# Expert stage of a decoder kernel: the transpose of a block's token rows placed directly ahead of the matmuls that read it

## The reference

```
choices = top 2 of 8 of (normed x) @ router_logits        # per token
gate_out = x_of_expert @ gating_einsum[e]                 # 512 -> 2 x 512
activation = gelu(gate_out[:, 0]) * gate_out[:, 1]
expert_outputs = activation @ linear[e] * per_expert_scale[e]
out = sum over the 2 chosen experts of weight * expert_outputs
```

## Time and profile before

| | us |
|---|---|
| median of 3 runs (2063.98 to 2066.97) | 2065.59 |
| the profiled execution's own time | 2066.97 |
| its span, first to last instruction | 2065.2 |
| TensorE busy | 1872.6 (91%) |
| VectorE busy | 1022.1 (49%) |
| ScalarE busy | 593.3 (29%) |
| expert blocks, from the first transposes to the last `dn` matmul | 1101.84 to about 1337.9 |

### The profile page before, as it was taken

How to read it: one execution, slowest core, us unless ns; L and a number is a source line. 1 busy time by engine, 2 the same in 40 slices (tenths; PEclk the granted TensorE clock), 3 DMA queues, 4 the chain that set the end, 5 groups by cost and what they waited for, 6 DMA issues and landing times.

```text
span 2065.2 us, 29153 instructions
## 1 busy us (share of the span) xinstructions
PE 1872.6 (91%) x11802; PEld 1218.9 (59%) x11802; DVE 1022.1 (49%) x1888; ACT 593.3 (29%) x1899; POOL 391.7 (19%) x456
## 2 busy tenths in 40 slices
PE   6799999999999999999866999958999999989898
PEld 5575656645666665665655888745766744434344
DVE  3555655426556655666730011046444543534599
ACT  0313222405455454555510111102122121212411
POOL 3332322320010110110011000052211200000488
PEclk9899999999999999999767999978999999999999
DMA  9000002000000000001045888740000205432010
GB/s 374 11 1 1 1 1 97 1 23 16 1 16 16 2 16 16 1 16 62 1 159 196 342 331 329 265 144 1 1 1 1 107 36 227 176 133 112 0 37 36
DMA packets 30821, 170.70 MB, mean 83 GB/s; under 512 B 3832, under 2 KB 3832, under 8 KB 17024
## 3 DMA queue, kind: packets, MB, share of 16 engines
q1 hardware_dynamic: 28128, 161.50, 20.7%
q0 software_dynamic: 2560, 7.34, 1.2%
HBM read 155.98 MB, written 16.52 MB: 84 GB/s over the span
## 4 chain that ended last, share of the span: by engine, by line
PE 74%; DVE 12%; issue 4%; DMA 4%; ACT 3%; POOL 3%; SPq 0%; POOLq 0%; DVEq 0%
PE PS L1109 7%; PE PS L897 6%; PE PS L946 5%; PE PS L1189 5%; PE PS L1149 5%; PE PS L986 4%; PE PS L977 4%; PE PS L1219 4%; PE PS L1118 3%; PE PS L954 2%; DMA R<-in_ctx 2%; PE PS L1009 2%; PE PS L1025 2%; PE PS L1045 2%; PE PS L1250 2%
## 5 line engine op out<-in xcount | busy, mean ns | idle before, releaser
L1987 POOL TENSOR_TENSOR rstd<-veps,mhalf 112x1 f32<-112x1 f32 (+1 forms) x76 | 57.6, 759 | 697.7 <-DVE veps L1279 683.4
L1109 PEld LDWEIGHTS PS<-R,W 128*128 128x128 f32 x1344 | 154.9, 194 | 11.6 <-issue 11.6
L1405 DVE TENSOR_REDUCE nmx<-PS 112x2 f32<-112x750 f32 x128 | 114.1, 933 | 91.6 <-PE PS L1009 91.6
L1109 PE MATMUL PS<-R,W 128*128 128x128 f32 x1344 | 155.2, 277 | 1.9 <-issue 1.9
L1808 ACT ACTIVATE R<-PS,small 112x112 f32<-112x112 f32 x256 | 87.0, 378 | 230.7 <-DVE small L1318 230.7
L1856 ACT ACTIVATE R<-PS,nmx 112x375 f32<-112x375 f32 x256 | 143.0, 575 | 1.3 <-DVE nmx L1405 1.3
L897 PE MATMUL PS<-xT,W 128*128 128x224 f32 x640 | 126.9, 356 | 0.0
L1350 DVE TENSOR_TENSOR x<-x,PS 112x512 f32<-112x512 f32 x40 | 27.5, 688 | 198.4 <-PE PS L1189 90.8
L897 PEld LDWEIGHTS PS<-xT,W 128*128 128x128 f32 x640 | 121.2, 192 | 5.8 <-issue 5.3
L2005 POOL TENSOR_TENSOR R<-R 128x224 f32<-128x224 f32 x80 | 52.8, 660 | 364.2 <-DVE R L1300 364.2
L1025 PE MATMUL PS<-cst,R 112*125 112x112 f32 x768 | 107.9, 286 | 13.0 <-DVE R L1418 9.2
(11 more groups left out here) (286 smaller groups left out, 3317.8 us busy)
## 6 DMA issues: line engine op xcount, KB each, us to landing
W<-in_we SPq DMA_DIRECT2D x63, 1024.0 KB, 7.1
W<-in_entwT SPq DMA_DIRECT2D x8, 1024.0 KB, 5.0
W<-in_entpw SPq DMA_DIRECT2D x8, 1024.0 KB, 7.4
W<-in_ctxT SPq DMA_DIRECT2D x8, 750.0 KB, 4.3
R<-in_ctxT SPq DMA_DIRECT2D x8, 750.0 KB
R<-in_ctx SPq DMA_DIRECT2D x8, 750.0 KB
xs_rows<-in_x SPq DMA_DIRECT2D x3, 1792.0 KB, 39.0
R<-xs_rows SPq DMA_DIRECT2D x21, 256.0 KB, 7.2
```

The costliest lines, as they stand in the source:

```text
L1109: o = e.matmul(PS[:, m, c * 128:(c + 1) * 128], gate_up(j % 3, k, off + c * 128), BT[:, j % 2, k, :], start=k == 0, stop=k == 3)
L1405: e.tensor_reduce(nmx[0:S, par, r:r + 2], PS[0:S, r:r + 2, 0:SC], AX.X, ALU.max, negate=True).then_inc(*up("cmax", (b, c, par, r)))
```

## The change

The step `bt` of a block moves from behind the `gu` of the block before it to directly ahead of the `gu` of its own block. Before, the steps of round j are `gu j`, `bt j+1`, `dn j-1`; now they are `bt j`, `gu j`, `dn j-1`. The load of the token rows moves too: it was issued behind the pair of `gu` loads (for block j+3), and is now issued behind the `dn` load (for block j+2). Which block waits for what, the buffers and their number, and the instructions themselves are unchanged.

```diff
     out += [("put", b) for b in range(NBATCH)] + [("load", "experts", 0)] + [("load", "rows", j) for j in range(3)]
-    out.append(("bt", 0))
     for j in range(NBLK + 1):
         if j < NBLK:
-            out += [("gu", j), ("load", "gu", j + 3)]
-        if j + 1 < NBLK:
-            out += [("bt", j + 1), ("load", "rows", j + 3)]
+            out += [("bt", j), ("gu", j), ("load", "gu", j + 3)]
         if j:
-            out += [("dn", j - 1), ("load", "dn", j + 2), ("load", "y", j - 1)]
+            out += [("dn", j - 1), ("load", "dn", j + 2), ("load", "rows", j + 2), ("load", "y", j - 1)]
         if j == NBLK - 2:
```

## The result

The changed kernel takes 2084.78 us (median of 4 runs, 2083.97 to 2086.59), the kernel before beside it 2065.24 us: 19.5 us more, a ratio of 1.0095 with a 95% interval of 1.0078 to 1.0113. It is slower, clear of the noise; predicted were 2085.9 us, with a range of 2080.5 to 2091.5.

What follows compares the result with a forecast made beforehand. TensorE alone was taken to pace the expert stage. 19 new waits of 1.07 us make 20.3 us, added to the median-based 2065.59 for 2085.9 us, slower by 1.0%; range 2080.5 to 2091.5.

Steps and rivals of the forecast that it cites:

- TensorE sets the pace, and nothing in the stage can be gained: Expert stage: TensorE alone paces it, 11.01 us per steady block; a stall between its groups adds in full.
- the bare waits of blocks 0 and 1: Stage start, no dn to cover the copy: TensorE idle 0.83 us before gu of block 0, 1.06 before block 1's.
- 19 waits of 1.07 us: Blocks 2 to 20: gu waits for VectorE's copy of the transposed rows, 1.07 us each, 20.3 us in all.
- One sign: Profile after, expert stage: the line of the copy would be shown as now waited for by TensorE.
- The loads of the token rows cost nothing: Loads issued behind dn weights: 11.7 us until needed, against landings of 7.0 to 8.6 before; no cost.
- the lighter queues: DMA in the stage: a block's 3.67 MB spread over 12.1 us, about 303 GB/s instead of 334.
- The end of the stage: After the last dn: TensorE's 27.65 us idle for last output rows, gather and mixing moves along; nothing counted.
- the third rival: Stage end gives time back: at best 8.2 us from the last write, 2077.7; all 0.01, a part 0.02.
- The clock: Expert stage: a wait of this length leaves TensorE's granted clock at 1.00.
- the rival: Clock falls in every block: 32.7 us on top over 19 blocks, 2118.6 us; chance 0.05.

Runs made afterwards that it cites:

- the last run: Kernel before with the second layer's last five weight loads behind the last output write and first gathers, and block 1's transposes ahead of block 0's gu: 2056.16 us.
- the pair of second copies: VectorE first copies the transposed rows to a spare tile: added to the kernel before, 2067.26 us; added to the changed kernel, 2100.24 us.
- the halves: Changed kernel with the copy made in two halves of 256 columns, gu starting when the first half is there: 2077.98 us.
- every second block: Kernel before with the transposes moved directly ahead of their gu for even blocks alone, ten of the 19: 2077.52 us, ratio 1.0058.
- the run with 3.73 us: Changed kernel with four spare copies ahead of the true one, lengthening TensorE's idle in each block: 2171.79 us, ratio 1.0521.
- the run with the write ahead: Kernel before with the last five loads of the second layer's weights issued behind the last output rows' write: 2061.17 us, ratio 0.9985.

## Why the prediction was right, point by point

*TensorE sets the pace, and nothing in the stage can be gained.* Right for the steady blocks: the loss in the stage, 20.25 us, is all in the result. "There is no wait in it that a better order could take away" was too much for the stage as a whole. The prediction itself read the bare waits of blocks 0 and 1, and the last run took 1.57 us out of the stage by order alone. On the change it has no bearing, since both kernels have these two waits.

*19 waits of 1.07 us.* Right, in sum and in parts: the chain 0.04 + 0.69 + 0.10 = 0.83 stands in the timeline to the hundredth; a block takes 12.09 us where 12.08 was worked out; 19 x 1.07 = 20.3 against 20.25. The idle of 0.83 us by itself is only part of a trip's price: taking the exposed latency of the transposes (0.16) and the slower start of `gu` (0.08, again 7.22 from its start to the next group's) into the term was worth it, since with the bare idle alone it would have been 15.8. These two are read from distances in the timeline; no run here varies them. The reason given for the 0.08, that weights can't be loaded ahead after a stop, fits the rows of the weight loads before the change: the first one of a steady `gu` starts 0.43 us ahead of its matmul (1125.40), that of block 1 0.03 us (1114.31):

```profile
1124.97 0.19 PEld L1109 LDWEIGHTS PS<-R,W 128*128 128x128 f32 x1 [0.24 <-issue]
```
```profile
1114.28 7.22 PEld L1109 LDWEIGHTS PS<-R,W 128*128 128x128 f32 x64 [1.27 <-issue]
```

That the 0.83 us are a wait for the copy, and neither the order nor VectorE's load, was shown by the pair of second copies and by the halves; that it goes block by block, by every second block. One sign did not come as it was written: the view names nobody as waiting for the copy's line and prints "issue", so the wait is read from the times.

*The loads of the token rows cost nothing.* Right for this change. In the changed kernel they land in 6.6 to 8.0 us (median 6.8), a little faster than the 7.0 to 8.6 (median 7.2) before. The argument from the lighter queues explains little of it by itself: with the transposes moved alone, so with lighter queues and the load at its old place, the median was 7.1, and with the load at the new place and the queues as full as before 8.3. Only both together gave 6.8. Issued at 1134.68 and needed at 1146.20, they had 11.5 us, where I had 11.7: the rows go out 0.57 us after the end of `dn` and not 0.4, and the prediction's own row already gave 0.5 (1125.59 + 0.33 - 1125.40). The reason holds only together with the moved transposes. By itself the same move costs 22 us, and of this the prediction said nothing, since it looked at the two moves together only; the first expectation on it was wrong.

*The end of the stage.* Right that it gives nothing back: 10.43 us for the last write after, 10.32 before, and TensorE's idle the same. But the part that the third rival called possible, 8.2 us from this write, is really there for another kernel, though not by the write alone.

*The clock.* Right for 0.83 us, at 1.00 from block 1 to the end of the stage. Transposes and a short idle in each of 21 blocks left the clock alone, also with 1.55 us; with 3.73 us it went down and up again, 15 blocks of 20. The Trainium skill says on the page "TensorE: Matmul & The Clock Gate" (section "A second HAM failure mode: psum-queue depth-cycling") that short idles between groups of matmuls can make the clock oscillate, and (section "Part 4: PE-mode transpose") that transposes do not count as busy in the same way. The outcome that the prediction drew from the two did not come about at this size; the run with 3.73 us shows what the first of them says. One argument against the rival had a wrong number: of a block's 12.1 us it is 7.14 + 3.43 = 10.6 that are dense matmuls, and not 9.5. With the right one the argument is a little stronger.

*The numbers.* 2084.78 against 2085.9; the measured difference to the runs beside it, 19.5, lies 0.8 under the 20.3, within the noise of medians that differ by up to 2 us between sets of runs of the same kernel (2064.46 to 2066.49). The stage, 20.25 against 20.3, is the better test of the term; that the medians came as close is in part luck. The range was widened for the noise by 1 us on either side, where the text says about 1.5; it decides nothing here.

## What to carry to other kernels

Where a result goes from TensorE through another engine and back to it, the order of TensorE's own list has to hold other work of at least the length of that trip; here it was 3.43 us of `dn` for a trip of 1.07. Price such a trip from a place where the trace shows it bare, which is often the first round of a loop, and take the distance between starts and not the "idle before" alone. A load has a deadline and not just a place in a queue: when its issue or its consumer moves, count again from issue to need, for each of the two moves by itself.

## What the hardware showed that was not expected

A DMA that is alone in the queues lands in 2.0 us (256 KB of output rows), and the same one behind 4 MB of weights in 10.3; whoever stands behind the weights pays, be it the write or the gather that follows it (11.30 us in the run with the write ahead). And a longer idle ahead of the first block can cost more than its own length: one more copy there made block 0's `gu` about 1.4 us longer (1100.15, 10.33 us, against 1100.91, 8.96 us), and 1.1 us in the kernel before. The clock rose later: windows over the same stretch show it, although `gu` had started 0.76 us earlier in the first of them:

```profile
1104.00:1108.00 4.00, 4.00 (x28) 4.00 (x28) 0.00 (x0) 0.60 (x1) 0.00 (x0) 0.71 0.00 0
```
```profile
1104.00:1108.00 4.00, 4.00 (x37) 4.00 (x36) 0.00 (x0) 0.60 (x1) 0.00 (x0) 0.97 0.02 4
```

The first is the changed kernel with the second copy, the second the changed kernel itself. It does not go by the length of the idle: with four spare copies (3.73 us ahead of `gu`) block 0's `gu` took 9.34 us, only 0.4 more than with none. What sets the moment at which the clock rises stays open.
